# Cross-attention scores straight from the context, through queries multiplied by transposed key weights, with the residual in a ring of six tiles

## The reference

```
q = x @ Wq          # x: layernorm of the input, 4096 x 256; Wq: 256 x 1024
k = context @ Wk    # context: 64 x 256 x 192;              Wk: 192 x 1024
v = context @ Wv
sim = jnp.einsum('bhid,bhjd->bhij', q, k) * SCALE
attn = jax.nn.softmax(sim, axis=-1)
out = jnp.einsum('bhij,bhjd->bhid', attn, v)
x = x + out.transpose(0, 2, 1, 3).reshape(B, Nq, INNER_DIM) @ Wo + bo
```

## Time and profile before

| | us |
|---|---|
| median of three runs | 2390.77 |
| lowest, highest | 2390.59, 2395.83 |
| the profiled execution | 2393.78 |
| its span, first to last instruction | 2392.0 |
| cross-attention, first to last start of a K matmul | 21.3 to 1279.3 |
| self-attention begins on VectorE | 1297.0 |

### The profile page before, as it was taken

The page is one execution under the profiler, slowest core; times in us unless marked ns, Lnnn a source line. Parts: engine busy times, 40 slices in busy tenths (PEclk is TensorE's granted clock), DMA queues, the critical chain, the costliest instruction groups (busy, mean ns, idle before and its releaser), DMA issues. The chain is left out here.

```text
span 2392.0 us, 53442 instructions
## 1 busy us (share of the span) xinstructions
PE 2264.0 (95%) x18144; PEld 1987.0 (83%) x18144; DVE 1552.6 (65%) x3393; ACT 1281.5 (54%) x3900; POOL 849.8 (36%) x1008
## 2 busy tenths in 40 slices
PE   5999999999999999999997999999999965999996
PEld 4888888888888888888886899999999953888885
DVE  5656665666566656665655798888989856445442
ACT  4555555555555555555553666666666631445442
POOL 3333333333333323332332122222222231777674
PEclk9999999999999999999998999999999985999998
DMA  5000000000000000000002000000000011444434
GB/s 174 19 10 18 9 18 9 18 17 10 13 14 18 9 18 9 18 9 18 9 1 71 1 13 16 18 9 18 9 18 18 10 45 42 102 80 95 86 52 104
DMA packets 52984, 74.09 MB, mean 31 GB/s; under 512 B 9424, under 2 KB 36816, under 8 KB 52848
## 3 DMA queue, kind: packets, MB, share of 16 engines
q1 hardware_dynamic: 39952, 55.07, 7.2%
q0 software_dynamic: 12960, 18.12, 4.5%
HBM read 55.60 MB, written 21.76 MB: 32 GB/s over the span
## 5 line engine op out<-in xcount | busy, mean ns | idle before, releaser
L356 POOL TENSOR_TENSOR p_sb<-p_sb,rinv 128x512 f32<-128x512 f32 x256 | 283.8, 1108 | 837.1 <-DVE rinv L606 837.1
L528 ACT ACTIVATE p_sb<-s_ps,nmax 128x256 f32<-128x256 f32 x512 | 237.9, 470 | 426.9 <-DVE nmax L587 426.9
L749 POOL TENSOR_TENSOR sp_sb<-sp_sb,srinv 128x512 f32<-128x512 f32 x128 | 133.1, 1040 | 428.4 <-DVE srinv L935 428.4
L58 DVE SCALAR_TENSOR_TENSOR qbd_lo<-m_ps,qbd_hi 64x256 fp32r<-64x256 f32 x256 | 108.1, 422 | 226.7 <-ACT qbd_hi L46 225.0
L57 DVE TENSOR_TENSOR kt_lo<-k_ps,kt_hi 128x512 fp32r<-128x512 f32 x256 | 176.1, 688 | 110.6 <-ACT kt_hi L45 109.0
L45 ACT CAST kt_hi<-k_ps 128x512 fp32r<-128x512 f32 x256 | 151.6, 592 | 130.7 <-PE k_ps L65 130.2
L883 ACT ACTIVATE sp_sb<-sm_sb,snmax 128x128 f32<-128x128 f32 x512 | 199.4, 390 | 7.0 <-DVE snmax L946 3.9
L603 DVE COPY pt_sb<-t_ps 128x512 f32<-128x512 f32 x256 | 176.6, 690 | 38.0 <-PE t_ps L449 34.2
L587 DVE TENSOR_REDUCE nmax<-s_ps 128x2 f32<-128x512 f32 x256 | 174.1, 680 | 0.3 <-PE s_ps L65 0.2
L449 PEld LDWEIGHTS t_ps<-ident,p_sb 128*128 128x128 f32 x1024 | 127.3, 140 | 34.9 <-issue 1.2
L449 PE MATMUL t_ps<-ident,p_sb 128*128 128x128 f32 x1024 | 153.3, 272 | 1.0 <-DVE pt_sb L603 1.0
(11 more groups left out here) (280 smaller groups left out, 7398.6 us busy)
## 6 DMA issues: line engine op xcount, KB each, us to landing
ctx_raw<-in_ctx_t SPq DMA_DIRECT2D x32, 256.0 KB, 2.8
ctx_raw<-in_ctx_t SPq DMA_DIRECT2D x64, 128.0 KB, 2.9
xn<-f_xn SPq DMA_DIRECT2D x16, 256.0 KB, 2.2
acc<-x_sb SPq DMA_DIRECT2D x16, 256.0 KB, 2.3
e_raw<-in_gate SPq DMA_DIRECT2D x8, 512.0 KB, 3.9
e_raw<-in_up SPq DMA_DIRECT2D x8, 512.0 KB, 4.8
e_raw<-in_down SPq DMA_DIRECT2D x8, 512.0 KB, 6.1
x_sb<-in_x SPq DMA_DIRECT2D x1, 3584.0 KB, 15.0
```

Source lines behind the costliest of these rows:

```text
L356: nc.gpsimd.tensor_tensor(prob, prob, inv, ALU.mult).then_inc(norm_done, 1)
L528: ex = nc.scalar.activation(p_sb[:, k, b * J:(b + 1) * J], s_ps[1 - w][:, b * J:(b + 1) * J], ACT.Exp, bias=nmax[:, k, b:b + 1], scale=1.0 ...
L749: nc.gpsimd.tensor_tensor(prob, prob, inv, ALU.mult).then_inc(norm_done, 1)
```

## The change

There is no key projection. With k = context Wk, the scores q k' of a head are (q Wk') context': the queries are multiplied by the transposed key weights of the head, 64 wide on one side and 192 on the other, and the scores are then taken from the context. This *absorption* is done once for a pair and a group, head by head: `absorb(m, pair, h)` issues four matmuls of 256 columns into the one PSUM tile `qk_ps` (128 context columns and the rest of 64, each with the high and the low part of the key weights; the queries' high and low parts stand in the two halves of `q_sb`, the key weights stand twice). ScalarE rounds `qk_ps` (128x512) into `qk_hi`, VectorE subtracts for the 128 columns (`qk_lo`) and for the rest (64 rows of `qk_hi`). The scores have five products instead of three. The pair that is absorbed in a step is the one that was projected in the step before: steps u=1, p=2 to 7 and u=0, p=0 and 1. In the first tile every step absorbs, and its values are computed ahead of it.

Further: the key weights are transposed at the start (16 copies on GpSimd, 32 transposes, eight rounds of rounding and subtraction); the context's rest is kept as `cr_hi`, `cr_lo` in full height; `x_sb` gives way to `x_ring`, three groups of two tiles, which SyncE loads and, once the bias is added, stores into `x_mid` in HBM; the self-attention loads `x_sb` from there, four tiles first; mask and blank rows are made in the self-attention's block, the other constants in the cross-attention's.

```diff
+            x_ring = sbuf(ph, "x_ring", [P, SLOTS, 2, D])
+            def absorptions(t, u, p, first, look, drain):
+                if first:
+                    return p
+                if u == 1 and p > 1 and look:
+                    return PAIRS * (t // 2 + 1) + p - 2
+                if u == 0 and p < 2 and not drain:
+                    return PAIRS * (t // 2) + PAIRS - 2 + p
+                return None
@@ SyncE
+                def load_x(g):
+                    wait(sp, s_kept, DMA * (g - SLOTS + 1))
+                    sp.dma_start(x_ring[:, g % SLOTS, :, :], x_dram[:, bass.ds(2 * g, 2), :]).then_inc(s_more, DMA)
+                def keep_x(g):
+                    sp.wait_ge(bo_added, 2 * g + 2)
+                    sp.dma_start(x_mid_rows[:, bass.ds(2 * g, 2), :], x_ring[:, g % SLOTS, :, :]).then_inc(s_kept, DMA)
@@ TensorE
+                def absorb(m, pair, h):
+                    wait(pe, q_done, m + 1)
+                    wait(pe, qk_done, 2 * m + h)
+                    for c in range(2):
...
+                        mm = three_pass(pe, qk_ps[:, c * 2 * P:(c + 1) * 2 * P], [
+                            (wkt_hi[:, cols], q_sb[:, pair % 2, h, :]), (wkt_lo[:, cols], q_sb[:, pair % 2, h, :])])
+                    mm.then_inc(qk_mm, 1)
-                            three_pass(pe, k_ps[:], hi_lo(wk_hi[:, c0], wk_lo[:, c0], cx_hi[:, u, :], cx_lo[:, u, :]) + [
-                                (wk_hi[:, c1], cx_rem[:, u, :]), (wk_lo[:, c1], cx_rem[:, u, :])]).then_inc(k_mm, 1)
+                                mm = three_pass(pe, s_ps[1 - w][:, keys], hi_lo(
+                                    main_hi, main_lo, cx_hi[:, up, keys], cx_lo[:, up, keys]) + [
+                                    (rest, cr_hi[:, up, keys]), (rest, cr_lo[:, up, keys])])
+                        if absd is not None:
+                            absorb(absd, p if first else (p - 2) % PAIRS, 1)
@@ ScalarE
+                def absorbed_hi(m, pair, h, used):
+                    act.wait_ge(qk_mm, 2 * m + h + 1)
+                    wait(act, s_mm, used)
+                    split_hi_act(nc, qk_hi[:, pair, :, :, h, :],
+                                 qk_ps[:].rearrange("p (c t q) -> p c t q", c=2, t=4)).then_inc(qk_hi_done, 1)
@@ VectorE
+                def absorbed_lo(m, pair, h):
+                    dve.wait_ge(qk_hi_done, 2 * m + h + 1)
+                    split_lo_dve(nc, qk_lo[:, pair, :, h, :], four(qk_ps[:, 0:2 * P]), qk_hi[:, pair, 0, :, h, :])
+                    rest = qk_hi[REM:P, pair, 1, :, h, :]
+                    split_lo_dve(nc, rest, four(qk_ps[REM:P, 2 * P:4 * P]), rest).then_inc(qk_done, 1)
@@ self-attention, SyncE
+                sp.dma_start(x_sb[:, 0:X_FIRST, :], x_mid_rows[:, 0:X_FIRST, :]).then_inc(s_mid[0], DMA)
```

More of the change, by code:

```diff
@@ L323, in _ @@
-                with sp.Fori(1, GROUPS) as g:
-                    for u in range(2):
-                        load(2 * g + u, u)
+                for u in range(2):
+                    load(2 + u, u)
+                with sp.Fori(2, GROUPS - 1) as g:
+                    load(2 * g, 0)
+                    keep_x(g - 2)
+                    load_x(g + 1)
+                    load(2 * g + 1, 1)
+                for u in range(2):
+                    load(TILES - 2 + u, u)
+                for g in range(GROUPS - 3, GROUPS):
+                    keep_x(g)
@@ L390, in turn_x, with values, turn_wk @@
                     mm.then_inc(xt_mm, 1)
+                def values(n, u, p):
+                    jt, half = p % 4, p // 4
+                    wait(pe, v_done, n)
+                    rows = slice(jt * P, (jt + 1) * P)
+                    c = slice(half * HALF, (half + 1) * HALF)
+                    three_pass(pe, v_ps[:], hi_lo(cx_hi[:, u, rows], cx_lo[:, u, rows], wv_hi[:, c], wv_lo[:, c]) + [
+                        (cr_hi[:, u, rows], wv_rem[:, c]), (cr_lo[:, u, rows], wv_rem[:, c])]).then_inc(v_mm, 1)
+                def turn_wk(pair):
+                    wait(pe, wk_done, pair - 1)
+                    pe.wait_ge(wk_dup, 2 * pair + 2)
+                    for h in range(2):
+                        for c in range(2):
+                            mm = pe.transpose(s_ps[pair % 2][:, (2 * h + c) * P:(2 * h + c + 1) * P],
+                                              wk_twice[:, pair % 2, c, h].rearrange("p r d -> p (r d)"), ident[:])
+                    mm.then_inc(wk_mm, 1)
                 def tile(t, u, first, last, look, drain=False):
@@ L479, in tile, with q_rows, four @@
                             turn_x(t // 2 + 1)
+                pe.wait_ge(s_const, CONSTS)
+                weights.wait_split(pe, V_SPLIT)
+                pe.wait_ge(s_ctx, 3)
+                pe.wait_ge(s_rem, 1)
+                values(0, 0, 0)
                 turn_x(0)
+                for p in range(1, 3):
+                    values(p, 0, p)
                 weights.wait_split(pe, Q_SPLIT)
                 pe.wait_ge(xt_done, 1)
+                project_q(0, 0)
+                for pair in range(PAIRS):
+                    turn_wk(pair)
+                    if pair + 3 < PAIRS:
+                        values(pair + 3, 0, pair + 3)
+                pe.wait_ge(wk_done, PAIRS)
                 run_tiles(pe, tile)
-            def heads(ps, qbd, pair, h):
-                r = slice(h * HEAD, (h + 1) * HEAD)
-                return (ps[r, 0:2 * P].rearrange("p (b q) -> p b q", b=4), qbd[r, pair, :, h * HEAD:(h + 1) * HEAD])
+            def q_rows(h):
+                return slice(h * HEAD, (h + 1) * HEAD)
+            def four(a):
+                return a.rearrange("p (t q) -> p t q", t=4)
             def o_half(p):
@@ L555, in tile @@
                             xt_hi_copy(t // 2 + 1)
-                xt_hi_copy(0)
                 for n in range(V_SPLIT):
                     weights.split_hi(act, n)
-                act.wait_ge(s_zero, 2)
+                keep_values(0, 0, 0)
+                xt_hi_copy(0)
+                for n in range(V_SPLIT, Q_SPLIT):
+                    weights.split_hi(act, n)
+                for p in range(1, 3):
+                    keep_values(p, 0, p)
+                q_hi(0, 0)
+                for pair in range(PAIRS):
+                    wk_hi_copy(pair)
+                    if pair + 3 < PAIRS:
+                        keep_values(pair + 3, 0, pair + 3)
                 run_tiles(act, tile)
@@ L635, in _ @@
                 xt_lo_copy(0)
-                for n in range(Q_SPLIT):
+                for n in range(V_SPLIT, Q_SPLIT):
                     weights.split_lo(dve, n)
-                rem_lo(0, 0)
-                for n in range(Q_SPLIT, V_SPLIT):
-                    weights.split_lo(dve, n)
-                dve.wait_ge(s_zero, 2)
+                q_lo(0, 0)
+                for pair in range(PAIRS):
+                    wk_lo_copy(pair)
                 run_tiles(dve, tile)
+        x_sb = sbuf(root, "x_sb", [P, TILES, D])
+        mask = sbuf(root, "mask", [P, 4, P])
+        blank = sbuf(root, "blank", [P, ROW])
+        s_mask, s_mid = sem("mask_ready"), [sem("s_x_first_loaded"), sem("s_x_rest_loaded")]
+        X_FIRST = 4
+        of_self = lambda g, u: x_sb[:, 2 * g + u, :]
         xn_sb = sbuf(root, "f_xn", [P, TILES, D])
```

316 lines of the change are left out of this document (172 added, 144 removed).

## The result

The changed kernel takes 2601.98 us, median of 4 runs (2595.78 to 2611.17), the kernel before 2392.5 us (2390.59 to 2395.83). The ratio is 1.087, 95% interval 1.0855 to 1.0891. It is slower by 209 us; 2599 was forecast, within 2515 to 2680.

What follows compares the result with a forecast made beforehand. TensorE's issue of matmul columns was taken as the bound. Absorbing steps 230, plain steps -88, first tile 12, start 7, phase change 7 and clock 40 sum to +208 on 2393.8 us: 2602 profiled, median 2599, range 2515 to 2680.

Steps and rivals of the forecast that it cites:

- The bound before: Cross-attention: TensorE bound by matmul columns issued; the 0.2 us wait at k_ps not taken as a guide for qk_ps.
- the loop: Absorbing steps followed by another: both halves share qk_ps, making a serial chain over three engines, 7.3 us a turn.
- rival 1: TensorE stays the bound: steps gain 53 us, start and phase change cost 14, 2352 us; chance 0.05.
- the start: Ahead of the first tile: key-weight loads, copies and transposes put the first step at 28 us for 21.3, +7.
- Absorbing and plain steps: Cross-attention behind the first tile: absorbing steps cost 230 us more, the 128 plain steps 88 us less.
- Weight loads: TensorE: three more a step, 146 us more on their row, but overlapping matmuls, so charged nothing.
- 2417: Weight loads: TensorE's saving shrinks to nothing, start and phase change add 26, about 2417 us; chance 0.02.
- Clock: TensorE's idles in the loop lower its granted clock, 1.2 us a fall, three in four of 45 idles: +40 us.
- Rival 4: The clock falls at nearly every wait, or slow matmuls idle the next step too: 2667 us and more; chance 0.15.
- rival 3: The loop as worked out, the clock staying at 2.4 GHz: 2559 us; chance 0.25.
- The first tile: First tile of the cross-attention, absorbing in every step without values: 54.5 us for 42.5, +12, bounds 8 to 16.
- Change of phase: Between cross-attention and self-attention: last residual rows stored and first four tiles loaded back, +7 us, bounds 4 to 10.

Runs made afterwards that it cites:

- e10: The changed kernel with e6's order, two banks for the absorbed queries and the output projection moved to step 5, ahead of that step's values: 2346.0 us.
- e3: The changed kernel with VectorE's copy of the transposed probabilities made twice in each absorbing step: 2678.4 us.
- e2: The changed kernel with ScalarE's copy of the values made twice in each absorbing step: 2614.9 us.
- e6: The changed kernel, same instructions and one bank, with the second half's absorption, rounding and subtraction and the query's rounding moved earlier in the queues: 2408.1 us.
- e9: The changed kernel with unread 512-column matmuls filling TensorE's waits, 10 in even steps and 5 in odd ones: 2571.5 us.
- e4: The changed kernel with a bank for each half of the absorbed queries, the output projection sharing the values' bank, queue order otherwise kept: 2519.3 us.
- e11: e10 with key weights loaded early and doubled by GpSimd and VectorE, and four of the first tile's value steps made inside that tile: 2344.1 us.
- e1: The changed kernel with unread 256-column matmuls filling TensorE's waits, 20 in even steps and 11 in odd ones: 2609.2 us.

## Why the prediction was right, and which terms were off

**The bound before: right.** TensorE's issue was the bound, and the 0.2 us at k_ps was no guide for qk_ps. e10 shows the other side of it: with the loop out of the way the change does bring what rival 1 had, 2346 for 2352. That the sums agree so well is luck: the start costs e10 14.6 us where rival 1 had 7, and a group gains 3.9 us where rival 1's 53 us make 3.3.

**The loop: right in place and size.** 7.3 us forecast from rows of before, 7.33 measured, in even steps and, where TensorE ran at full clock, in odd ones. Its links came at 0.77, 1.39, 2.29, 3.02, 3.93, 4.73, 5.62, 6.35 and 6.43 us after the first matmul; forecast were 0.75, 1.34, 2.22, 2.90, 3.85, 4.65, 5.54, 6.26 and 6.43. That it is a chain of orders was a reading of the code; e3, e2 and e6 show it. The point from which rival 1 decides, a loop no longer than TensorE's own work, was reached in e10 by the same instructions in another order and another bank: the rows of the loop were serial only by the order of the queues, which "I see none that isn't ordered by the code" took as given.

**Absorbing and plain steps: right.** A plain step takes 2.78 and 4.06 us (2.8 and 4.05 forecast), a group without slow clock 88.2 us in e9 (88.5 forecast). TensorE's own work in an absorbing step, 4.5 and 5.7 us forecast, is 4.49 and 5.74 in e10.

**Weight loads: right to charge none.** TensorE's weight loads fell to 79% of the span in the changed kernel; in e10 they stand at 85%, and an absorbing step, which has seven loads more than before, takes what its columns take. The three loads a step are a mean: a plain step has one less. The 146 us that they were to add to the row of weight loads are 7.5 in e10 (1987.0 to 1994.5 us). By the Trainium skill's section Identifying the Most-Contended Engine (Perfetto Trace Analysis), which judges headroom by that row, 2417 was a rival; here the trace doesn't bear it out, as e10's absorbing steps show. What the Trainium skill's section Matmuls (Perfetto Trace Analysis) says on rotating banks agrees with the trace for this tile: e4's second bank took 83 us off. It is not the larger part: e6 took 194 off with one bank.

**Clock: right in kind, a little large.** 40 us forecast, 30.5 measured by e9 (32 by the periods). The forecast had 34 falls of 1.2 us, three in four of 45 waits. Measured are 30 of 44: 22 turns of 8.3 us in the mean (8.0 to 9.3), about 1.0 more than at full clock, and 8 that cost 1.5 at the end of a group's absorptions. Rival 4 is out, and rival 3 (no clock cost) with it.

**The start: mis-sized, +15.7 for +7, outside its bounds of 2 to 13.** The step that failed is "Values of tile 0 (8 x 1.16) hide there under the loads". They begin at 14.09, when VectorE has split the value weights and the context's rest, and five of them stand on TensorE between the rounds of the key weights, 1.26 us each: 6.3 of the 14.1 us from the first round (22.89) to the first absorption (37.01). They aren't the whole of it: e11 has one of the five there, and its rounds still take 11.5 us. The forecast priced GpSimd's copies, but GpSimd waited for TensorE, 1.35 us a round. The forecast gave no sum for its 28 us, so which of the other steps it had too short stays open.

**The first tile: mis-sized, +18.4 for +12**, just beyond its bound of 16. Its turns were priced at full clock; from 37 to 98 us the granted clock was 0.78. In e6 it is 60.7 us from the tile's first absorption to the next tile's, for 69.2 in the changed kernel, so the new order takes 8.6 us of it away.

**Change of phase: right** (+5.7 for +7). **The rest: 0 forecast, +4.8 measured, and not the change's.** Its largest part lies in the experts, where from the first to the last matmul into `e_g_ps` it is 349.9 us for 344.8 before. But in e3, e4, e6 and e10, with the same code there, it was 344.7, 344.5, 344.9 and 347.5, in e1 351.3; the other five lie between 344.4 and 348.1. It varies from one execution to the next.

That the total came within 3 us, 2602 for 2599, is luck, since the errors cancel: start and first tile 15 us more than forecast, the steady part 13 less, of which some 9 are the clock and 4.5 the group (88.2 for 88.5, 15 times).

## What to carry to other kernels

Here a result that needs trips over three engines, twice a step, cost the sum of what stood in each queue ahead of it, not the work. Before pricing an edit by columns or busy shares, write the turn down engine by engine; and when it is the bound, first move its links (here the second half's absorption, rounding and subtraction, and the query's rounding) ahead of what nobody waits for so soon, and then look for a second buffer; here the order was worth 194 us and the buffer 16 more. A bank borrowed for that brought its own waits: place its other user where it has been free for long.

## What the runs showed of the hardware that was not expected

- Filling waits of 2.6 and up to 1.6 us with 512-column matmuls nobody reads raised the granted clock in the cross-attention to 1.00, from 0.94 to 0.97 in stretches of 200 us, and took 30 us off a kernel that is bound by a loop over three engines. In that loop TensorE's own part is short, but a turn at the lower clock was still about 1.0 us longer.
- In the changed kernel behind its first tile, TensorE ran on at the lower clock (256-column matmuls 0.21 us apart, not 0.12) behind 30 of the 44 waits of 2.6 to 2.8 us, and behind none of 1.61 us or less.
- The same fill with twice as many instructions of half the width lost it all: at the jump back to the loop's head TensorE stood still 13 times for about 2 us with no releaser that the profile shows.
